# Cross-attention and a mixture of experts on one core: weight loads, splits and one wait moved between queues and engines

## The reference

```
x = x + xattn(layernorm(x), ctx)      # x (32, 112, 256), ctx (32, 375, 192)
x = x + ffn(layernorm(x))

xattn: q = x Wq (16 heads of 64); k, v = ctx Wkv
       softmax(q k^T / 8) v, heads joined, then Wproj (1024 -> 256) + bproj
ffn:   softmax router over 8 experts, the best 2 of each token, shares normalised;
       expert e: (silu(x Wgate_e) * (x Wup_e)) Wdown_e, with 512 hidden columns
```

## Time and profile before

| what | value |
|---|---|
| time, median of 3 runs | 1544.87 us (1543.21 to 1544.89) |
| the profiled execution: its time, its span | 1544.89 us, 1541.6 us |
| busy: PE, PEld, DVE, ACT, POOL | 96%, 84%, 62%, 47%, 36% of the span |
| mean granted TensorE clock | 0.986 |
| first matmul; first expert tile's matmul | 12.09 us; 1202.41 us |

### The profile page before, as it was taken

The page is one execution under the profiler, slowest core; times in us unless marked ns, Lnnn a source line. Parts: engine busy times, 40 slices in busy tenths (PEclk is TensorE's granted clock), DMA queues, the critical chain, the costliest instruction groups (busy, mean ns, idle before and its releaser), DMA issues. The chain is left out here.

```text
span 1541.6 us, 37314 instructions
## 1 busy us (share of the span) xinstructions
PE 1479.3 (96%) x11882; PEld 1295.8 (84%) x11883; DVE 953.7 (62%) x2580; ACT 729.9 (47%) x2030; POOL 549.0 (36%) x635
## 2 busy tenths in 40 slices
PE   6999999999999999999999999999984899999997
PEld 5788888888888888888888888888873688888886
DVE  5667777677767676776767676677665533333332
ACT  4555555555555555555555555555544222222222
POOL 3234333343423343333434332424247123232322
PEclk9999999999999999999999999999997899999999
DMA  6522222222222222222222222220027233323332
GB/s 185 144 65 66 71 67 74 67 70 64 76 64 87 81 83 70 64 75 65 73 64 70 70 76 77 70 94 29 27 65 263 50 54 48 54 48 55 48 53 26
DMA packets 101099, 113.73 MB, mean 74 GB/s; under 512 B 17244, under 2 KB 88140, under 8 KB 101068
## 3 DMA queue, kind: packets, MB, share of 16 engines
q1 hardware_dynamic: 88444, 96.43, 20.4%
q0 software_dynamic: 12144, 15.66, 6.3%
q10 hardware_dynamic: 480, 1.24, 0.3%
HBM read 61.37 MB, written 51.93 MB: 73 GB/s over the span
## 5 line engine op out<-in xcount | busy, mean ns | idle before, releaser
L793 ACT ACTIVATE prob<-bank,neg_max 112x375 f32<-112x375 f32 x512 | 295.3, 587 | 141.3 <-DVE neg_max L1054 141.3
L1054 DVE TENSOR_REDUCE neg_max<-bank 112x1 f32<-112x375 f32 x512 | 243.8, 539 | 18.2 <-PE bank L1289 18.2
L1299 PE MATMUL bank<-ident,prob 112*125 112x112 f32 x1536 | 216.4, 275 | 14.3 <-ACT prob L793 14.0
L1299 PEld LDWEIGHTS bank<-ident,prob 112*125 112x125 f32 x1536 | 197.1, 189 | 26.2 <-ACT prob L793 17.1
L732 POOL DMA_INDIRECT out<-y_out,dest_now x63 | 97.8, 1552 | 243.8 <-ACT y_out L882 214.7
L918 DVE TENSOR_TENSOR K_l<-bank,K_h 128x376 fp32r<-128x376 f32 x256 | 140.5, 550 | 66.4 <-ACT K_h L753 63.9
L1323 PE MATMUL bank<-probT,V 125*64 125x112 f32 x3072 | 177.6, 265 | 3.3 <-DVE probT L1060 2.6
L1197 PE MATMUL bank<-Wgu,hT_h 128*128 x504 | 176.0, 431 | 1.5 <-DVE hT_l L1154 1.5
L1323 PEld LDWEIGHTS bank<-probT,V 125*64 125x64 f32 x3072 | 149.9, 138 | 29.9 <-issue 24.0
L1175 DVE COPY hidT<-bank 128x512 f32<-128x512 f32 x63 | 43.5, 691 | 172.9 <-PE bank L1497 172.9
L908 DVE COPY V<-bank 125x512 f32<-125x512 f32 x96 | 66.4, 692 | 134.8 <-PE bank L1261 131.7
(11 more groups left out here) (174 smaller groups left out, 3517.7 us busy)
## 6 DMA issues: line engine op xcount, KB each, us to landing
bins<-pad_rows SPq DMA_DIRECT2D x29, 1032.0 KB, 5.8
inv_rows<-sums SPq DMA_DIRECT2D x126, 128.0 KB, 2.8
Wgu<-in_L_ffn_gate_up_w SPq DMA_DIRECT2D x8, 1024.0 KB, 6.3
h_in<-bins SPq DMA_DIRECT2D x63, 129.0 KB, 2.1
y_sb<-in_ctx SPq DMA_DIRECT2D x32, 187.5 KB, 2.7
y_sb<-in_ctx SPq DMA_DIRECT2D x62, 93.8 KB, 2.7
x_sb<-in_x SPq DMA_DIRECT2D x16, 224.0 KB, 2.9
x_res<-in_x SPq DMA_DIRECT2D x32, 112.0 KB, 2.5
```

Of the source, the lines that this page charges most:

```text
L793: nc.scalar.activation(prob[:, j, :], S_ps[j][0:LQ, 0:LKV], ACT.Exp, bias=neg_max[:, j:j + 1], accum_out=row_sum[:, head // HB, head % HB: ...
L1054: nc.vector.tensor_reduce(neg_max[:, j:j + 1], S_ps[j][0:LQ, 0:LKV], AX.X, ALU.max, negate=True).then_inc(max_done, 1)
L1299: last = nc.tensor.transpose(S_ps[j][0:KR, t * LQ:t * LQ + LQ], prob[:, j, t * KR:t * KR + KR], ident[0:LQ, 0:LQ])
```

## The change

- SP no longer waits for the arrival of Wk's first part before it issues the load of Wq.
- Both parts of Wproj are now made by POOL, ahead of its loop over pairs, in one cast and one subtraction of 128x2048; ACT's cast (L842) and DVE's subtraction (L1111) are gone.
- SP issues expert 3 and the 3 MB of Wd at the end of item 31's body, behind the store of item 30's rows. ACT issues experts 4 and 5 in step 3 of item 31, and 6 and 7 in the body after it.
- ACT's cast of expert 3 moves out of item 31, step 1, into the body after it and is made together with that of expert 4; that of expert 5 comes after the pairs; those of 6 and 7 come behind the cast of the first tile's rows (`hi_of_rows(0, 0)`).
- DVE's subtraction of expert 3 moves from step 3 of item 31 to step 1 of the body after it.
- POOL's split of expert 2 moves from behind that of expert 1 to behind the scatter of item 29.
- ACT's one-column silu (tile `table`), the first use of that function, is gone.
- `project` waits for both halves of an item's output before its first matmul, where it waited for each half in turn.

```diff
@@ sync
             load_x(0)
-            sp.wait_ge(wk_in, 16)
             sp.dma_start(wq[:], Wq.rearrange("(k p) n -> p k n", p=P)).then_inc(wq_in, 16)
@@ sync, pair
                         load_expert(sp, 2)
-                        sp.wait_ge(made, a.n0 + len(a.items))
-                        load_expert(sp, 3)
-                        sp.dma_start(Wd[:, early:E]...).then_inc(wd_in, 16)
-                    if known(i) and i == NP and not odd:
-                        sp.wait_ge(scores_made, B * H)
-                        for e in (4, 5):
-                            load_expert(sp, e)
-                        sp.wait_ge(pv_made, B * NS)
-                        for e in (6, 7):
-                            load_expert(sp, e)
...
+                    if known(i) and i == NP - 1 and odd:
+                        sp.wait_ge(made, a.n0 + len(a.items))
+                        load_expert(sp, 3)
+                        sp.dma_start(Wd[:, early:E]...).then_inc(wd_in, 16)
@@ gpsimd
             split_y(1, 1, None)
+            pool.wait_ge(wp_in, 16)
+            pool.tensor_copy(wp_hi, wp[:]...).then_inc(wp_done, 1)
+            pool.wait_ge(wp_done, 1)
+            pool.tensor_tensor(wp_lo, wp[:]..., wp_hi.bitcast(F32), ALU.subtract).then_inc(wp_done, 1)
...
                         split_expert(1)
-                        split_expert(2)
...
                         scatter(b - 2, odd, (i, i - 1 + odd))
+                    if known(i) and i == NP - 1 and odd:
+                        split_expert(2)
@@ scalar
-                        if known(b) and b == 0 and s == 1:
-                            act.wait_ge(wp_in, 16)
-                            nc.scalar.copy(WpH..., wp...).then_inc(wp_done, 1)
-                        if known(i) and i == NP - 1 and odd and s == 1:
-                            hi_of_experts(3, 4)
+                        if known(i) and i == NP - 1 and odd and s == NS - 1:
+                            act.wait_ge(scores_made, B * H)
+                            for e in (4, 5):
+                                load_expert(act, e)
                         if known(i) and i == NP and not odd and s == 0:
-                            hi_of_experts(4, 7)
+                            act.wait_ge(pv_made, B * NS)
+                            for e in (6, 7):
+                                load_expert(act, e)
+                            hi_of_experts(3, 5)
...
-            hi_of_experts(7, E)
-            nc.scalar.activation(table[:], ident[:, 0:1], ACT.Silu)
+            hi_of_experts(5, 6)
...
             hi_of_rows(0, 0)
+            hi_of_experts(6, E)
@@ vector
-                        if known(b) and b == 0 and s == 3:
-                            dve.wait_ge(wp_done, 1)
-                            nc.vector.tensor_tensor(WpL..., wp..., WpH..., ALU.subtract).then_inc(wp_done, 1)
-                        if known(i) and i == NP - 1 and odd and s == 3:
+                        if known(i) and i == NP and not odd and s == 1:
                             lo_of_expert(3)
@@ tensor, project
+                pe.wait_ge(OT_lo, 2 * b + 2)
                 if known(b) and b == 0:
                     pe.wait_ge(wp_done, 2)
-                for half in range(2):
-                    pe.wait_ge(OT_lo, 2 * b + half + 1)
-                    for j in range(HALF * half, HALF * half + HALF):
...
+                split_product(C_ps[0:LQ, 0:C], [(OT_h[:, j, :], OT_l[:, j, :], WpH[:, j, :], WpL[:, j, :])
+                                                for j in range(NJ)]).then_inc(proj_made, 1)
```

More of the change, by code:

```diff
@@ L295, in attention_and_experts @@
         inv_top = sb("inv_top", [LQ, 1], F32)
-        table = sb("table", [P, 1], F32)
         wd_at = base + size - E * FJ * C * 4
@@ L510, in pair @@
                         load_expert(sp, 2)
-                        sp.wait_ge(made, a.n0 + len(a.items))
-                        load_expert(sp, 3)
-                        sp.dma_start(Wd[:, early:E].rearrange("p e k n -> p (e k) n"),
-                                     down_w[early:E].rearrange("e (k p) n -> p (e k) n", p=P)).then_inc(wd_in, 16)
-                    if known(i) and i == NP and not odd:
-                        sp.wait_ge(scores_made, B * H)
-                        for e in (4, 5):
-                            load_expert(sp, e)
-                        sp.wait_ge(pv_made, B * NS)
-                        for e in (6, 7):
-                            load_expert(sp, e)
                     if there(b - 1, B):
@@ L534, in pair @@
                         load_x(i + 2)
+                    if known(i) and i == NP - 1 and odd:
+                        sp.wait_ge(made, a.n0 + len(a.items))
+                        load_expert(sp, 3)
+                        sp.dma_start(Wd[:, early:E].rearrange("p e k n -> p (e k) n"),
+                                     down_w[early:E].rearrange("e (k p) n -> p (e k) n", p=P)).then_inc(wd_in, 16)
             over_pairs(sp, pair, 1, NP - 3)
@@ L676, in _ @@
             split_y(1, 1, None)
+            wp_hi, wp_lo = (t[:].rearrange("p k n -> p (k n)") for t in (WpH, WpL))
+            pool.wait_ge(wp_in, 16)
+            pool.tensor_copy(wp_hi, wp[:].rearrange("p k n -> p (k n)")).then_inc(wp_done, 1)
+            pool.wait_ge(wp_done, 1)
+            pool.tensor_tensor(wp_lo, wp[:].rearrange("p k n -> p (k n)"), wp_hi.bitcast(F32), ALU.subtract).then_inc(wp_done, 1)
             def pair(i):
@@ L839, in pair @@
                             evacuate(a, k)
-                        if known(b) and b == 0 and s == 1:
-                            act.wait_ge(wp_in, 16)
-                            nc.scalar.copy(WpH[:].rearrange("p k n -> p (k n)"),
-                                           wp[:].rearrange("p k n -> p (k n)")).then_inc(wp_done, 1)
-                        if known(i) and i == NP - 1 and odd and s == 1:
-                            hi_of_experts(3, 4)
+                        if known(i) and i == NP - 1 and odd and s == NS - 1:
+                            act.wait_ge(scores_made, B * H)
+                            for e in (4, 5):
+                                load_expert(act, e)
                         if known(i) and i == NP and not odd and s == 0:
-                            hi_of_experts(4, 7)
+                            act.wait_ge(pv_made, B * NS)
+                            for e in (6, 7):
+                                load_expert(act, e)
+                            hi_of_experts(3, 5)
             over_pairs(act, pair)
-            hi_of_experts(7, E)
-            nc.scalar.activation(table[:], ident[:, 0:1], ACT.Silu)
+            hi_of_experts(5, 6)
             act.wait_ge(plan, N_PLAN)
@@ L1108, in pair @@
                             low_part(a, k)
-                        if known(b) and b == 0 and s == 3:
-                            dve.wait_ge(wp_done, 1)
-                            nc.vector.tensor_tensor(WpL[:].rearrange("p k n -> p (k n)"), wp[:].rearrange("p k n -> p (k n)"),
-                                                    WpH[:].rearrange("p k n -> p (k n)").bitcast(F32),
-                                                    ALU.subtract).then_inc(wp_done, 1)
-                        if known(i) and i == NP - 1 and odd and s == 3:
+                        if known(i) and i == NP and not odd and s == 1:
                             lo_of_expert(3)
```

## The result

The changed kernel takes 1551.59 us (median of 5 runs, 1551.01 to 1553.63) against 1544.87 us (1542.42 to 1545.18) of the kernel before in the same rounds: a ratio of 1.0051, with a 95% interval of 1.0036 to 1.0065. It is 6.7 us slower by the medians, 7.9 us by the ratio. The forecast was +7.3 us, 1552.2 us. The profiled execution took 1553.44 us around its span of 1551.2 us, 1.9 us above the median, and its span is 9.6 us longer than that of the kernel before, so its rows show a loss 2 to 3 us larger than the times do. The kernel before was run 62 times more beside the experiments; its medians there are 1546.88 and 1546.91 us, 2.0 us above its profiled execution.

What follows compares the result with a forecast made beforehand. PE, 96% busy, was taken as the bound, with POOL's unbroken series the path at the end of attention. Start +6.4, dent -1.0, tail +1.6, first tiles +0.3 gave +7.3 us, 1552.2 us, range 1548 to 1556.

Steps and rivals of the forecast that it cites:

- gap before q4: At the start, PE stands still before q4 because DVE's WvU ends late: 4.0 us, from 3.1 to 4.2.
- half clock behind it: After PE's idle before q4, a half-rate stretch costs 2.4 us, from 1.7 to 3.2.
- dent at 70 us: PE's idle at 70 to 75 us goes as DVE's Wproj subtraction leaves item 0: -1.0 us.
- SP's wait: At the start, issuing Wq's load sooner costs 0; PE's first matmul may shift by -0.5 to +1.0 us.
- POOL's series to OT_l: End of attention, POOL's work from expert 1 to OT_l: 22.4 us long, against 24.66 before.
- OT_l to residual: Last projection of item 31: 24 matmuls at half clock, 5.1 us, plus 0.3 before the residual.
- first tiles: After attention, ACT's two casts and the table load delay the gate of tile 1: +0.3 us, at most +1.6.
- The lock at the start: POOL's Wproj subtraction gets its turn between DVE's WvL and WvU and holds WvU up: +6.4 us, +3.1 to +7.4.
- The cover of ACT's cast: Removing ACT's Wproj cast gains nothing, as DVE's other work sets PE's wait for probT; uncovered, up to 1.9 us.
- The tail: End of attention to residual: OT_l 2.0 us sooner, projection slower, residual +1.6 us, bounds -0.7 to +4.4.
- the lock did not bite there: Rival at the end: DVE's low part of expert 3 comes between OT_h and OT_l, +2.3 us, 1554.5 us; chance 0.05.
- The new wait of the projection: Item 31's projection waits for both halves, so its first 12 matmuls no longer run ahead; 24 take 5.1 us.

Runs made afterwards that it cites:

- run 62: Not a label but a count: the kernel before was run 62 times more beside the experiments, with medians of 1546.88 and 1546.91 us.
- e1: Kernel before with one edit, both parts of Wproj made by POOL ahead of its loop: 1551.68 us against 1546.88, ratio 1.0034.
- e2: Kernel before with one edit, SP's wait for Wk ahead of the load of Wq removed: 1548.35 us, ratio 1.0009.
- e3: Kernel before with all edits at the end of attention and in the first tiles, none at the start: 1547.95 us, ratio 1.0012.
- e4: Changed kernel with POOL making Wproj's parts only after DVE's low parts of Wv: 1547.70 us, ratio 1.0007 to the kernel before.
- e6: e3 with the projection waiting for its halves in turn again: 1546.58 us, ratio 0.9997 to the kernel before.
- e7: e3 with POOL's split of expert 2 behind item 31's last output half, DVE's low part of expert 3 one step later: 1547.29 us, ratio 1.0004.
- e5: Kernel before with only ACT's cast of expert 3 and DVE's low part of it moved behind the last attention step: 1547.90 us against 1546.91, 1.0003.
- e8: Kernel before, Wproj on POOL behind Wv, expert 3's cast later, POOL's expert 1 behind item 29's scatter, expert 2 after OT: 1540.21 us, ratio 0.9951.

## Why the prediction was right

| term | predicted | measured |
|---|---|---|
| gap before q4 | 4.0 us | 4.03 (after), 4.04 (e1) |
| half clock behind it | 2.4 us | 2.6 (after), 1.7 (e1), each from q4 to the first scores less 5.40 |
| dent at 70 us | -1.0 us | not shown to come from the edit |
| SP's wait | 0 | first matmul +2.3 us; the time +1.4 (e2) |
| POOL's series to OT_l | 22.4 us | 22.39 (after), 22.44 (e3) |
| OT_l to residual | 5.4 us | 5.37 (after), 4.53 (e3) |
| first tiles | +0.3 us | +0.4 behind hT_h, +0.5 ahead of it |
| sum | +7.3 us | +6.7 us by the medians, +7.9 by the ratio |

**The lock at the start** is right in mechanism, place and size. POOL got its turn between WvL and WvU, as L608 had shown in the earlier trace rows. e1 does it alone, and e4 takes it away by moving POOL's work behind WvU. The clock's part lies in the range given. The cover of ACT's cast also held: nothing appears at its old place.

**SP's wait** is the term that was mis-sized: 0, with bounds of -0.5 to +1.0, and it is outside them, with +2.3 us at the first matmul and +1.4 us in the time. The step that failed is its ground that the load of Wq stands behind x on the same queue and that every byte is still to be moved. It named the right thing two sentences later, the tail of Wk beside it on ACT's queue, and gave it too little: loads that nobody yet needs were under way at the same time as the one that is waited for.

**The dent** went from 70 us, as forecast, but that is not the edit's gain. Between the first scores and item 2 (k = 4 of the list) the shift falls from 8.07 to 7.27 in the changed kernel. It also falls in e2, where DVE still has Wproj, from 34.00 - 31.97 = 2.03 to 1.25. In e4 it grows, from 2.14 to 3.07, behind a stretch of low clock at 60 to 65 us. In e3, which changes nothing here, it goes from 0.10 to 1.45, more than the term. What is lost in this stretch changes its place from kernel to kernel.

**The tail** came out as reckoned in the changed kernel: -2.3 us for POOL's series and +3.6 for the projection, where the terms were -2.0 and +3.6. In e3 the second is only +2.8. The hold of 2.28 us on the scatter's issue was real: without a DVE subtraction beside them the issues take 0.94 to 1.15 us in every run. Here the rule weighed in the prediction ("SBUF — State Buffer", section "Who interferes with whom", in the Trainium skill) is not borne out: the page infers that such a subtraction would not hold the issue, but beside it the issue took 3.25 us, and the measurement decides. DVE's low part of expert 3 came behind OT_l, at 1186.41, so the lock did not bite there. The new wait of the projection cost what was said, and in e6's trace 1.5 us of it are back.

**The sum** is near the measured one partly by luck. The parts measured by e1, e2 and e3 are 5.3, 1.4 and 1.9 us, 8.6 together, where the terms were 5.4, 0 and 1.9. The missing 1.4 us of SP's wait is smaller than the interval of the whole, 0.0036 to 0.0065 or 5.6 to 10.0 us. That is why the total does not show it and e2 was needed. Something else hid part of it. The sum was laid on one base, as if the 3.3 us by which the time exceeds the span would stay. They do not: by the medians of the runs the time exceeds the span by 2.0 to 2.2 us in the changed kernel, e3, e4 and e7, and by 3.0 to 3.2 us in the kernel before, e1, e2, e5, e6 and e8. e6 and e3 differ in the projection alone, so the 1.1 us come of that edit; what happens in them no run shows. Within the spans e1, e2 and e3 add 4.6, 1.7 and 2.2 us, and 8.5 together are 1.2 more than the forecast.

**Open** is how much of the missing gains is the clock of PE and how much the order of DVE's small operations. e7's trace shows both, and no run separates them; in e5's, PE is late for O_now and for the residual, and what the clock alone costs is untested. Why expert 1 lands 7.27 us later when the last item but one is only 6.13 us late was not tried either.

## What to carry to other kernels

A long wait of the busiest engine is not the path until the engine that feeds the next step has been followed too: here taking out 13 us of ACT's waiting was worth nothing, and a version that gives POOL's wait to work that others need, with other edits beside it, gained 7.6 us. Before a long SBUF operation is moved to POOL, look at what DVE does in the same microseconds, and put it beside operations that read a bank; the same move cost 5.3 us in one place, and 5 us later no cost of it is seen. A wait ahead of a load may be there to keep the queue clear for another load, so look at what that other one feeds before the wait is taken out.

## What the hardware showed unexpectedly

- A load can be delayed by loads on another engine's queue. With Wq, Wv, Wproj and parts of the context issued by 6.3 us on SP's queue in place of 9.3, the second part of Wk, on ACT's, was there 2.4 us later (its cast starts at 11.97 against 9.61 us; in all traces at 11.97 to 12.48 without the wait and 9.55 to 11.15 with it). The next issue on SP then took 7.24 and 7.78 us, against 3.68 before.
- The turn-taking of POOL and DVE also stops operations of two columns that read one tile in SBUF: a cast of 112x2 took 3.06 us in the changed kernel, and in e7 a tensor_scalar of 112x2 took 4.53 us, each beside a POOL subtraction of 4.5 to 4.6 us. The same two took 0.27 and 0.22 us in e8 at 1187 us, away from any subtraction of POOL.
- A first use of silu behind the table load cost 1.28 us and no more: the load began at 1214.17, and the silu started at 1215.46.
- Where PE's idle time became longer (14.02 us in e5 for 10.76 before) and ended later, its clock was low for work that had run at full rate: 24 matmuls took 2.51 us in place of 1.37, at a granted clock of 0.50 from 1172 to 1183 us where it had been 1.00.
